# Counting a graph's edges in windows of 32 targets by 8 source blocks, with bias products on GpSimd

## The reference, cut to what matters

```python
h = maximum(layernorm(x), 0)
q, k, v = h @ Wq + bq, h @ Wk + bk, h @ Wv + bv
a = q @ k.T / sqrt(512)
a = a * adj + (1 - adj) * -1e6          # adj[src, dst] = 1 for every edge
x = x + softmax(a) @ v
h = maximum(layernorm(x), 0)
# graph convolution over the edges and a loop at every node;
# deg = edges into a node, dinv = deg ** -0.5, w = dinv[src] * dinv[dst]
g = agg(h @ W1 + b1)                    # segment sum of w * g[dst] over src
g = relu(batchnorm(g) * gamma + beta)
x = x + agg(g @ W2 + b2)
```

## Time and profile before

| | |
|---|---|
| median of 3 runs | 311.49 us (311.35 to 312.01) |
| the profiled execution | 311.82 us |
| its span, first to last instruction | 309.8 us |
| TensorE, weight loads, VectorE busy | 95%, 73%, 68% |
| ScalarE, GpSimd busy | 46%, 18% |
| TensorE's granted clock | 0.999 |

### The profile page before, as it was taken

One profiled execution on the slowest core, in us unless ns is written; L12 is line 12 of the kernel. 1 busy time (PEld: TensorE's weight loads), 2 busy tenths in 40 slices (PEclk: granted clock), 3 DMA queues, 4 the chain that ended last, 5 costly groups with the idle time before them and its releaser, 6 DMA issues.

```text
span 309.8 us, 4740 instructions
## 1 busy us (share of the span) xinstructions
PE 295.1 (95%) x1319; PEld 227.4 (73%) x1319; DVE 210.2 (68%) x470; ACT 143.6 (46%) x245; POOL 55.4 (18%) x96
## 2 busy tenths in 40 slices
PE   2999969899999999999999999999999999999995
PEld 2977436565666688888888888888788888888884
DVE  3787999999997747667647575757444288376311
ACT  1799944443445626635465445437632035233000
POOL 5234280000000170032121212203010043100000
PEclk9999999999999999999999999999999999999999
DMA  7707040000420127832834636133203000000221
GB/s 268 291 3 204 1 135 0 3 0 0 150 57 3 33 36 107 200 85 53 136 69 102 135 46 124 36 68 59 44 0 70 1 0 2 0 0 2 101 103 68
DMA packets 42310, 21.65 MB, mean 70 GB/s; under 512 B 35760, under 2 KB 36016, under 8 KB 42288
## 3 DMA queue, kind: packets, MB, share of 16 engines
q1 hardware_dynamic: 41744, 20.33, 26.9%
q10 hardware_dynamic: 544, 1.05, 0.9%
HBM read 10.88 MB, written 2.10 MB: 42 GB/s over the span
## 4 chain that ended last, share of the span: by engine, by line
PE 79%; DVE 10%; issue 4%; DVEq 4%; DMA 1%; ACT 1%; SPq 0%; ACTq 0%
PE ps L948 18%; PE ps L950 18%; PE ps L949 18%; PE ps L1196 9%; PE ps L1119 8%; PE ps L1018 5%; DVE src_oh L668 4%; PE ps L986 2%; DVEq L668 2%; DVE dst_oh L670 2%; DMA edge_i<-src_in 1%; DVE hT L651 1%; DVEq L670 1%; DVEq L660 0%; DVEq L674 0%
## 5 line engine op out<-in xcount | busy, mean ns | idle before, releaser
L668 DVE TENSOR_SCALAR src_oh<-iota,ecol 128x512 f16 x149 | 44.2, 346 | 4.0 <-issue 2.9
L1018 PE MATMUL ps<-src_oh,dst_oh 128*128 x149 | 37.9, 382 | 5.4 <-DVE dst_oh L670 4.6
L1018 PEld LDWEIGHTS ps<-src_oh,dst_oh 128*128 x149 | 14.4, 103 | 25.6 <-issue 16.7
L1119 PE MATMUL ps<-cnt,qh 128*128 128x512 f32 x128 | 30.1, 391 | 0.3 <-ACT cnt L541 0.3
L1196 PE MATMUL ps<-qh,cnt 128*128 128x512 f32 x128 | 29.3, 390 | 0.0
L443 ACT ACTIVATE cnt<-ps 64x512 int16<-64x512 f32 x32 | 18.9, 592 | 20.7 <-PE ps L1032 20.3
L1119 PEld LDWEIGHTS ps<-cnt,qh 128*128 128x128 f32 x128 | 23.9, 188 | 5.6 <-DVE qh L827 0.7
L1196 PEld LDWEIGHTS ps<-qh,cnt 128*128 128x128 f32 x128 | 23.9, 188 | 5.2 <-DVE vb L929 0.3
L950 PE MATMUL ps<-v,pT 128*128 128x512 f32 x64 | 25.0, 390 | 0.0
L948 PE MATMUL ps<-v,pT 128*128 128x512 f32 x64 | 24.9, 390 | 0.0
L949 PE MATMUL ps<-v,pT 128*128 128x512 f32 x64 | 24.9, 390 | 0.0
(11 more groups left out here) (176 smaller groups left out, 658.8 us busy)
## 6 DMA issues: line engine op xcount, KB each, us to landing
xt<-x_in SPq DMA_DIRECT2D x16, 256.0 KB, 3.3
out<-xt SPq DMA_DIRECT2D x8, 256.0 KB, 2.1
qk_raw<-L_gnn_Wk_in ACTq DMA_DIRECT2D x2, 512.0 KB, 4.9
qk_raw<-L_gnn_Wq_in SPq DMA_DIRECT2D x2, 512.0 KB, 6.7
wB_raw<-L_gnn_Wv_in SPq DMA_DIRECT2D x2, 512.0 KB, 8.9
wB_raw<-L_gnn_W_in SPq DMA_DIRECT2D x2, 512.0 KB, 4.3
w_raw<-L_gnn_W_in SPq DMA_DIRECT2D x2, 512.0 KB, 4.8
bias_row<-L_gnn_b_in SPq DMA_DIRECT2D x2, 256.0 KB, 3.7
```

The lines of the kernel that those rows point to most:

```text
L668: dve.tensor_scalar(src_oh[:, bass.ds(slot, 1), j, :].rearrange("p a n -> p (a n)"), iota[:, :], ecol[:, bass.ds(c + j, 1)], None, ALU.is_ ...
L1018: m = pe.matmul(ps[:, i % 2, :], dst_oh[:, bass.ds(slot, 1), :, j].rearrange("p a n -> p (a n)"), src_oh[:, bass.ds(slot, 1), j, :].rearra ...
L1119: m = pe.matmul(bank(g), qh[:, d, a, c * P:(c + 1) * P], cnt[:, d, n * HALF:(n + 1) * HALF], start=(d == 0 and a == 1), stop=last)
```

## The change

- Windows are 32 targets wide (NWIN = 32). Two of them (PAIR) form a group, and fill the two halves of one PSUM bank. There are still 16 groups, in the same ORDER.
- A one-hot of keys, `key_oh`, has 256 columns: source block (8) by target in the window (32). `src_oh` has the 128 places of the source in its block, one instruction per round. The product's rows are source places, its columns the keys.
- The straight pair of chunks is gone: each window is one loop, three chunks a round. Each group reads two bounds. The ring has 8 rounds. The targets need no shifting on GpSimd: the window is taken off by a constant in the comparison.
- The counts come out with sources on partitions (`cntT`), so masking reads them directly. All eight blocks are transposed by DMA into `cntD`, four ahead of p's first transposes and four behind them; ScalarE sums `cntD` into the degrees in attention's iterations 1 and 2, VectorE finishes them in iteration 3, and the loops are added in iteration 4.
- The products with bias rows (9) and with w (8) are GpSimd's; ScalarE sums each by a copy in place. w is made four groups earlier. The fill level is made once, for all rows, behind the last sum, and SP's first count transpose waits for it (the counts' place was that of rows used there).
- W2 goes where W1 was: it is loaded after the last product with W1 and split behind the attention loop on ScalarE and VectorE.
- Three small VectorE operations more prepare the edges.

```diff
-WIN = 64
-NW = N // WIN
-LEAD = 2
+WIN = 32
+NWIN = N // WIN
+PAIR = 2
+NW = NWIN // PAIR
+BLK = 8
+KEYS = BLK * WIN
 UNROLL = 3
-RING = 4
+RING = 8
...
-             [("q", 0, 1)], [("q", 0, 2)], [("q", 0, 3)], [], [("w", 0, 0)]]
+             [("q", 0, 1), ("w", 0, 0)], [("q", 0, 2)], [("q", 0, 3)], [], []]
...
             if t == 0:
-                sp.wait_ge(S["c16"], 2 * NW)
-            if t >= ADJ:
-                sp.wait_ge(S["masked"], t - ADJ + 1)
-            sp.dma_start_transpose(adj[:, t % ADJ, :].rearrange("p (b n) -> p b n", b=NT),
-                                   cnt16[:, t, :, :].rearrange("p b n -> p (b n)")).then_inc(
-                S[f"adj_in{t % ADJ}"], 16)
+                sp.wait_ge(S["c16"], NW)
+                sp.wait_ge(S["fill_ready"], 1)
+            sp.dma_start_transpose(cntD[:, :, t, :], cntT[:, t, :]).then_inc(S["turned"], 16)
...
+            if t == 0:
+                for u in range(KC, NT):
+                    turn_counts(u)
             if XT <= t + 3 < NT:
                 load_x(NT + t + 3)
-            if t == 0:
-                load_w(2)
...
+        sp.wait_ge(S["w1_ps"], NT)
+        load_w(2)
...
+        for n in (K, Q):
+            for k in range(KC):
+                pool.tensor_tensor(qk_raw[:, n, k, :], qk_raw[:, n, k, :], bias_row[:, n, :],
+                                   ALU.mult).then_inc(S["bias_products"], 1)
+        pool.wait_ge(S["bias_products"], 2 * KC)
+        pool.tensor_tensor(bias_row[:, 0, :], bias_row[:, 0, :], bias_row[:, 1, :], ALU.mult).then_inc(S["bias_products"], 1)
+        pool.wait_ge(S["item_hi"], nth(("w", 0, 0)))
+        for t in range(NT):
+            pool.tensor_tensor(row_of(t), row_of(t), w_row[:, :], ALU.mult).then_inc(S["row_products"], 1)
...
+            act.activation(cntT[:, :, targets].rearrange("p b (w t) -> p w b t", w=PAIR),
+                           ps[:, i % 2, :].rearrange("p (w b t) -> p w b t", w=PAIR, b=BLK), ACT.Copy).then_inc(S["c16"], 1)
...
+                act.activation(row, row, ACT.Copy, accum_out=total).then_inc(S["uw_ready"], 1)
...
+                act.activation(row_of(t), row_of(t), ACT.Copy, accum_out=hw[:, 0, t:t + 1]).then_inc(S["hw_sums"], 1)
...
+            return [dve.value_load(lohi[0:1, win:win + 1], min_val=256, max_val=257 * NCH)
+                    for win in (PAIR * ORDER[i], PAIR * ORDER[i] + 1)]
 
         def onehots(i, bounds):
 
-            first, end = bounds & (NCH - 1), bounds >> 8
-            dve.wait_ge(S["drel_ready"], i + 1)
-            chunks_of(i, first, LEAD)
-            with dve.Fori(first + LEAD, end, UNROLL) as c:
-                chunks_of(i, c, UNROLL)
+            for a in range(PAIR):
+                win = PAIR * ORDER[i] + a
+                with dve.Fori(bounds[a] & (NCH - 1), bounds[a] >> 8, UNROLL) as c:
+                    k = dve.snap(made, min_val=0, max_val=ROUNDS)
+                    slot = k & (RING - 1)
+                    dve.wait_ge(S["onehots_used"], k + 1)
+                    for j in range(UNROLL):
+                        dve.tensor_scalar(key_oh[:, bass.ds(slot, 1), j, :].rearrange("p a n -> p (a n)"), iota[:, :],
+                                          kcol[:, bass.ds(c + j, 1)], -float(KEYS * win), ALU.subtract, ALU.is_equal)
...
+            for a in range(PAIR):
+                with pe.Fori(bounds[a] & (NCH - 1), bounds[a] >> 8, UNROLL):
```

More of the change, by code:

```diff
@@ L286, in turn_h2 @@
             sp.dma_start_transpose(h16T[:, part, :, :], h16[:, part, :]).then_inc(S[landed], 16)
-        for t in range(ADJ):
+        for t in range(KC):
             turn_counts(t)
@@ L487, in _ @@
             counts(i)
+            if 4 <= i <= 8:
+                column_sums(range(2 * i - 8, min(2 * i - 6, 2 * KC + 1)))
+            if i >= NW - 3:
+                row_sums(range(2 * (i - NW + 3), 2 * (i - NW + 3) + 2))
             if i == 1:
@@ L571, in _ @@
                 hi_of(("q", 1, 3))
+                degrees(range(KC))
+            if i == 2:
+                degrees(range(KC, NT))
             if i == NT + 1:
@@ L644, in lo_of @@
             if what == "w":
[L645 removed]
+                dve.sem_inc(S["item_lo"], 1)
             elif what == "q":
@@ L697, in times_w_row @@
-        def times_w_row(blocks):
-            for t in blocks:
-                ins = dve.scalar_tensor_tensor(out=row_of(t), in0=row_of(t), scalar=1.0, in1=w_row[:, :], op0=ALU.mult,
-                                               op1=ALU.mult, accum_out=hw[:, 0, t:t + 1])
-            return ins
-        def mask_level(blocks):
-            if blocks.start == 0:
-                dve.wait_ge(S["uw_ready"], 4)
-                dve.wait_ge(S["item_lo"], nth(("w", 0, 0)))
-            else:
-                dve.wait_ge(S["hw_second"], 1)
-            step(dve.tensor_scalar(hw[:, 1, blocks], hw[:, 0, blocks], bqbk[:, 0:1], -1.0, ALU.add, ALU.mult))
-            dve.tensor_scalar(fill[:, blocks], hw[:, 1, blocks], NEG / SCALE, None, ALU.add).then_inc(S["fill_ready"], 1)
+            return [dve.value_load(lohi[0:1, win:win + 1], min_val=256, max_val=257 * NCH)
+                    for win in (PAIR * ORDER[i], PAIR * ORDER[i] + 1)]
@@ L714, in _, with mask_level @@
+        def mask_level():
+            step(dve.tensor_scalar(hw[:, 1, :], hw[:, 0, :], bqbk[:, 0:1], -1.0, ALU.add, ALU.mult))
+            dve.tensor_scalar(fill[:, :], hw[:, 1, :], NEG / SCALE, None, ALU.add).then_inc(S["fill_ready"], 1)
         early = list(start)
@@ L744, in _, with degrees @@
             onehots(i, now)
-            if 6 <= i <= 9:
-                columns_of_biases(K if i < 8 else Q, (0, 1) if i % 2 == 0 else (2, 3))
-        for i in range(NW - 2, NW):
-            for item in ahead[i]:
-                lo_of(item)
-        mask_level(slice(0, KC))
-        dve.wait_ge(S["c16"], 2 * NW)
-        step(dve.scalar_tensor_tensor(out=deg[:, :], in0=degp[:, 0, :], scalar=1.0, in1=degp[:, 1, :], op0=ALU.add,
-                                      op1=ALU.add))
-        dve.tensor_reduce(degm[:, 0:1], deg[:, :], AX.X, ALU.max).then_inc(S["degm_ready"], 1)
-        dve.sem_inc(S["deg_ready"], 1)
-        lo_of(("q", 1, 0))
+        lo_of(("q", 1, 0))
+        dve.wait_ge(S["hw_sums"], NT)
+        dve.wait_ge(S["uw_ready"], 2 * KC + 1)
+        mask_level()
+        dve.wait_ge(S["c16"], NW)
+        def degrees():
+            dve.wait_ge(S["deg_sums"], NT)
+            dve.tensor_scalar(deg[:, :], degp[:, :], 1.0, None, ALU.add).then_inc(S["deg_ready"], 1)
+            dve.wait_ge(S["deg_ready"], 1)
+            dve.tensor_reduce(degm[:, 0:1], deg[:, :], AX.X, ALU.max).then_inc(S["degm_ready"], 1)
         def large_flag():
@@ L847, in _ @@
                 mask_and_max(i)
-                add_loops(i)
+            if i == 3:
+                degrees()
+            if i == 4:
+                for b in range(NT):
+                    add_loops(b)
+            if i == 5:
+                large_flag()
             if 3 <= i < NT:
@@ L1009, in bounds_of @@
         def bounds_of(i):
[L1010 to L1022 removed]
+            return [pe.value_load(lohi[0:1, win:win + 1], min_val=256, max_val=257 * NCH)
+                    for win in (PAIR * ORDER[i], PAIR * ORDER[i] + 1)]
         def counts(i, bounds):
             if i >= 2:
[L1027 to L1031 removed]
+                pe.wait_ge(S["c16"], i - 1)
+            pe.matmul(ps[:, i % 2, 0:32], zerob[:, :], zerob[:, 0:32], start=True, stop=False, skip_group_check=True)
+            for a in range(PAIR):
+                with pe.Fori(bounds[a] & (NCH - 1), bounds[a] >> 8, UNROLL):
+                    k = pe.snap(used, min_val=0, max_val=ROUNDS)
+                    slot = k & (RING - 1)
+                    pe.wait_ge(S["onehots"], k + 1)
+                    for j in range(UNROLL):
+                        m = pe.matmul(ps[:, i % 2, a * KEYS:(a + 1) * KEYS],
+                                      src_oh[:, bass.ds(slot, 1), :, j].rearrange("p a n -> p (a n)"),
+                                      key_oh[:, bass.ds(slot, 1), j, :].rearrange("p a n -> p (a n)"), start=False,
+                                      stop=False, skip_group_check=True)
+                    m.then_inc(S["onehots_used"], 1)
+                    pe.reg_add(used, used, 1)
             pe.matmul(ps[:, i % 2, 0:32], zerob[:, :], zerob[:, 0:32], start=False, stop=True,
```

221 lines of the change are left out of this document (85 added, 136 removed).

## The result

The changed kernel takes **343.96 us** (342.89 to 344.43, 4 runs), the kernel before, beside it, 311.42 (311.30 to 312.01, 4 runs): ratio 1.1036, 95% interval 1.1007 to 1.1065. It is slower, as forecast, but by 32.5 us and not by 18; the range ended at 337. The profiled execution's span is 341.1 us against 309.8.

The account below looks back on a forecast made before the run. The counting stage was taken as bound by VectorE's sequencer, 1.15 us a round. From 311.8: +15.7 stage, +2.0 W2, 0 transposes, +0.3 start, -0.3 narrower first products, giving 329.5 us; range 319 to 337.

Parts of the forecast that it names:

- Work moved off VectorE: Counting stage: moving nine bias and eight row products to GpSimd gains 0; GpSimd's slowing of VectorE costs 0, at most 1 us.
- The lateness of the sums: Closing warning: a chain of 17 products and sums that comes late would make the forecast wrong, delaying fill and first softmax.
- The round is the sequencer's: VectorE's one-hot loop: its sequencer sets the round, which stays at 1.15 us though key rows get narrower.
- The engine's own round: VectorE's one-hot loop: with 256-column key rows the engine itself needs 0.91 us a round, before 1.12.
- The stage without the bursts: Counting stage: more reads, loop starts and rounds plus coupling add 15.7 us, with ends of 8 and 21.
- Its thirteen groups: Counting stage behind the third group: 45 rounds and group changes take 70.6 us on VectorE's sequencer, before 58.2: +12.4.
- The term of 1.5 for the coupling of the two engines: Counting stage: VectorE's and TensorE's equally slow issuing chains wait for each other, +1.5 us, bounds 0 and 5.
- width decides: Rival: VectorE's engine, not its sequencer, sets the counting rounds, so narrower rows make the kernel faster, 306 us; chance 0.05.
- the queue hides the reads: Rival: VectorE's sequencer runs ahead, so added reads and loop starts of thirteen groups cost half: 321.5 us; chance 0.15.
- TensorE's issuing is the slower chain: Rival: each group's item, reads and starts on TensorE lie in line with the rounds, +5: 335 us; chance 0.16.
- W2: Convolution: W2 loads later into W1's place, its splits delay the batch norm and z: +2.0 us, bounds 0.5 and 4.
- Transposes and degrees: Attention: eight count transposes on SP's queue and ScalarE's degree sums cost 0, bounds 0 and 2 us.

Follow-up runs that it names:

- experiment 11: Changed kernel, GpSimd products kept; key rows of 259 columns read from seven rows of 37 with a gap: 331.14 us, ratio 1.0624.
- experiment 1: Changed kernel with its 17 products back on VectorE and GpSimd's additions of bv held until the last counts: 329.94 us, ratio 1.0583.
- experiment 4: Experiment 1 with this graph's window bounds as constants, loops kept, no reads of bounds on either sequencer: 314.75 us, ratio 1.0097.
- experiment 6: Experiment 1 with constant bounds and every round written out on both engines, no loops: 311.34 us, ratio 0.9995.
- (10): Kernel before, with constant bounds and rounds written out on both engines: 309.52 us, ratio 0.9942.
- experiment 2: Kernel before, with only its nine bias products moved to GpSimd and summed by ScalarE: 318.92 us, ratio 1.0231.
- (7): Changed kernel with only the nine bias products on GpSimd; row products on VectorE, additions of bv wait: 337.05 us, ratio 1.0808.
- experiment 5: Experiment 1 with key rows and counting products 128 columns wide instead of 256, half the counts left out: 330.30 us, ratio 1.0594.

## Why the prediction was wrong

| kernel | last q item starts | time, median |
|---|---|---|
| before | 104.2 | 311.4 |
| changed | 133.3 | 344.0 |
| changed, one-port key rows (11) | 121.2 | 331.1 |
| products on VectorE (1) | 120.3 | 329.9 |
| that, constant bounds (4) | 105.0 | 314.8 |
| that, no loops (6) | 101.7 | 311.3 |
| before, no loops (10) | 101.9 | 309.5 |

**The step that failed** is "Work moved off VectorE": "I take 0. The upper end ... 1 us". It measured 14.0 us by the medians. In the two profiled executions it is 12.1: the last q item starts 133.3 - 120.3 = 13.0 us later and is itself 1.0 shorter. Three errors lie in it. First, it priced the contention from the shifts of targets, 128x132 in f16 and 0.7 us each, as a tenth of a microsecond per key row, and took that for the price under products of 128x512 in float32 as well. Under those a one-hot is held for one GpSimd instruction's length, 1.25 us. In eleven microseconds of burst VectorE completes nine one-hots; at four in 1.16 us it would be 39. Second, it set the slack of 0.24 us a round against the added time; against rounds of 5.0 us that slack is nothing, and catching up at 0.92 us a round gives back only as much as the sequencer had issued ahead: behind the first burst the changed kernel's branches come 5.8 us later than experiment 1's, and at 108 us still 5.5. Third, it counted only what moves to GpSimd, not what was there already: the additions of bv slid from behind the counts into them.

That it is the bursts is shown from both sides: take them away and the 14.0 us go (1); put one on the kernel before and it loses 7.3 (2); leave all of them and change only the key rows' shape, and 12.8 come back (11). The lateness of the sums, the warning with which the prediction ends, is not it: experiment 11 keeps their whole chain, and the time behind the first scores is 203.7 us with it and 203.6 without (7). The Trainium skill, SBUF — State Buffer, section SBUF: two separate sides, says that VectorE and GpSimd share a port pair under an exclusive lock: whichever starts first, a two-port or two-input VectorE instruction or a GpSimd one, keeps it for its whole length. The rows under 512-column GpSimd instructions agree: one one-hot for each 1.25 us and for each 0.61, 340 ns for the shape of experiment 11, 0.74 us for a low part that reads PSUM. The rows under the shifts of the kernel before do not:

```profile
L668 DVE TENSOR_SCALAR src_oh<-iota,ecol x14: 354/378/455, 39.7 to 45.3; 128x512 f16 x14
```

GpSimd made eight shifts of 0.66 to 0.91 us in that time, so two one-hots passed for each, and none was held for a shift's length, though the same rows were held for 1.3 us in experiment 2. Measured, then, the hold was a whole instruction's length for 512 columns and not for 132; no run here shows where between them it changes, or why. So the shifts could not give the price of the products.

**Right, and shown:**
- The round is the sequencer's, 1.16 us (forecast 1.15), with 256 columns or 128: experiment 5. The engine's own round is 0.92 (forecast 0.91): experiment 6. With free issuing the new layout gives 311.3 and the old 309.5, so issuing costs the new one 18.6 us and the old one 1.9.
- The stage without the bursts: +16.1 us by the last q item of experiment 1, forecast +15.7. Its thirteen groups, from the third group's last branch to the last one, take 117.1 - 45.4 = 71.7 us, forecast 70.6. The reads are the larger part (experiment 4, 15.2 us). The term of 1.5 for the coupling of the two engines was enough.
- The rival "width decides" falls with experiment 5 (330.3 us, against 306), and "the queue hides the reads" with experiments 1 and 4 (329.9, against 321.5). "TensorE's issuing is the slower chain" would have given 335; in experiment 1 TensorE still waits 11.1 us for VectorE's one-hots, so it is not the slower one there. Its issuing was not changed by itself in any run.

**Mis-sized:** W2 at +2.0. Everything from the products with the counts on costs about 0.5 us more than before, and TensorE's one wait for z is 0.25; the loads were issued in 0.45 us each where the earlier trace rows had 1.1 (those stood behind two transposes), and the first g was 0.1 us late, not 2.2. Transposes and degrees at 0 lie within the other 0.4 or so of the 0.9.

**Not priced:** the clock. In 45 to 60 us of the changed kernel the granted clock is 0.58, near the lower level of 1.2 GHz, after a stretch in which TensorE was busy for 6.71 of 14 us. Most of that is hidden, since VectorE sets the pace. It shows on the last q item: 4.1 us in the changed kernel, 125.4 - 120.3 = 5.1 in experiment 1, 106.7 - 101.7 = 5.0 in experiment 6, against 2.8 before. In the last two nearly all its products run at the lower clock; in experiment 1 TensorE had been busy for 8.3 of the 14 us up to 120:

```profile
122.59 0.63 PE L950 MATMUL ps<-hT,M 128*128 128x512 f32 x1
```

(TensorE of experiment 1.) So experiment 1's span of 329.0 us is made of 309.8 + 16.1 for the stage + 2.2 for the clock + 0.8 for the rest. The forecast's 329.5, next to its median of 329.9, had 15.7 and 2.0: the W2 term stood where a clock term belonged, so that the two totals meet so closely is partly luck. The same 2.2 us are why the new layout without loops is no faster than the old one without loops, though its q item starts 0.2 us earlier.

How much of the last 6.9 us is the row products' and how much the additions of bv's was not tried apart.

## What to carry to other kernels

Before work is moved to GpSimd, look at what VectorE does in the same microseconds: if that is 16-bit one-source or two-source work like these one-hots and GpSimd's instructions are long ones (512 columns of float32 here), count one GpSimd instruction's length for each VectorE instruction that starts during the burst, and count the GpSimd work that slides into the stretch as well. Short instructions elsewhere in the trace (132 columns here) do not give that price, and a burst may be short enough to cost nothing (5.6 us here, against 11.4 that cost 5.7). An operand shape that GpSimd does not hold up gives back nearly as much as moving the work back: 12.8 us against 14.0. And ask of a busy engine whether its instructions or its issuing set the round: narrower tiles buy nothing in a loop whose branches stay at their distance, and in these loops each register operation more in a round cost about 0.08 us.

## What the runs showed of the hardware that I had not expected

- While GpSimd ran 512-column float32 products (1.25 us each), VectorE's 16-bit key rows completed one per product: 1219 to 1301 ns instead of a spacing near 0.2. With one-input GpSimd operations (0.61 us) it was again one for one. Under shifts of 132 columns (0.68 us) it was not: two one-hots passed for each.
- The same comparison on 259 columns, read in seven rows of 37, was not held at all: 336 to 343 ns. It costs 0.06 us more than the 281 of the 256-column row where GpSimd rests; in the first burst the loop's branches kept their 1.16 us all the same.
- GpSimd's products were themselves slowed there, 11.15 us for eight against 10.00, in the trace of experiment 11.
- Bounds that are taken apart by shifts were worked out again in every round, though put into registers first: two operations and about 0.16 us a round.
